# First attention of a two-block model on one core: order of a step, place of the heads' output, running sums as two float32r matmuls

## The reference, cut to what matters

```
h   = w[cond] applied to x over the 32 tokens          # (64, 32, 256)
q,k = rope(h Wq'), rope(h Wk')                          # 16 heads of 128
v,g = h Wv', h Wg'
s   = clip(h Ws1' Ws2' + b, -32, 32)                    # 16 heads x 64 slots
z   = cumlogsumexp(s over tokens);  es = exp(s);  enz = exp(-z)
A   = causal(q k') / sqrt(128)
ok  = enz * (A es)
p   = softmax(ok);   W2 = causal((p*enz) es')
o   = W2 v;   o = o / sqrt(mean(o*o) + eps) * gn * silu(g)
x   = x + o Wo'
```

## Time and profile before

| | us |
|---|---|
| runs of the kernel | 1489.26, 1491.48, 1494.16; median 1491.48 |
| the profiled execution, its own time | 1494.37 |
| its span, first to last instruction | 1492.5 |
| busy in the span: TensorE / VectorE / ScalarE / GpSimd | 1361.8 / 918.0 / 507.1 / 514.6 |
| mean granted TensorE clock | 0.968 |

### The profile page before, as it was taken

One profiled execution on the slowest core, in us unless ns is written; L12 is line 12 of the kernel. 1 busy time (PEld: TensorE's weight loads), 2 busy tenths in 40 slices (PEclk: granted clock), 3 DMA queues, 4 the chain that ended last, 5 costly groups with the idle time before them and its releaser, 6 DMA issues. The chain is left out here.

```text
span 1492.5 us, 46698 instructions
## 1 busy us (share of the span) xinstructions
PE 1361.8 (91%) x19926; PEld 1060.2 (71%) x19926; DVE 918.0 (62%) x1825; ACT 507.1 (34%) x1123; POOL 514.6 (34%) x544
## 2 busy tenths in 40 slices
PE   2999999999999999999996598999999689997996
PEld 2677777777777777777764486777777567775664
DVE  2777777777777777777764465242433335665886
ACT  2344443444443444333342313132322222222332
POOL 0655545555544555544432212221212111122111
PEclk9999999999999999999999699999999879997998
DMA  6000000000001000000000510000000540000620
GB/s 200 9 13 13 14 16 13 27 13 13 13 16 28 13 13 13 3 2 3 2 2 2 201 52 1 0 0 0 0 1 0 167 121 1 0 0 3 197 66 22
DMA packets 33414, 47.57 MB, mean 32 GB/s; under 512 B 6718, under 2 KB 22296, under 8 KB 32728
## 3 DMA queue, kind: packets, MB, share of 16 engines
q1 hardware_dynamic: 31048, 42.69, 9.2%
q10 hardware_dynamic: 2112, 2.10, 0.5%
q0 software_dynamic: 80, 0.26, 0.1%
HBM read 42.68 MB, written 2.36 MB: 30 GB/s over the span
## 5 line engine op out<-in xcount | busy, mean ns | idle before, releaser
L233 POOL TENSOR_TENSOR rstd<-mse,mhalf 128x4 f32<-128x4 f32 x64 | 65.1, 1017 | 238.5 <-DVE mse L651 238.5
L563 ACT ACTIVATE ex<-ok,mn 128x64 f32<-128x64 f32 x256 | 68.2, 337 | 193.7 <-DVE mn L680 193.7
L403 PE MATMUL AW_TA<-w_o,ogT_s 128*128 128x256 f32 x512 | 129.0, 395 | 0.7 <-ACT ogT_s L488 0.7
L822 POOL TENSOR_TENSOR hT_lo<-h,hT_hi 128x512 fp32r<-128x512 f32 x44 | 56.8, 1292 | 192.8 <-ACT hT_hi L995 192.8
L228 POOL TENSOR_TENSOR turned<-t1c,t2s 128x512 f32<-128x512 f32 x62 | 79.8, 1287 | 117.5 <-DVE t2s L611 117.5
L626 DVE SCALAR_TENSOR_TENSOR gs<-gs,PJ 128x512 f32<-128x512 f32 x64 | 44.0, 687 | 122.5 <-ACT gs L504 122.5
L622 DVE RECIPROCAL enz<-SC 128x128 f32<-128x128 f32 x128 | 112.6, 921 | 4.7 <-PE SC L354 4.7
L303 PE MATMUL PJ<-hs_hi,w_hi 128*128 128x512 f32 x248 | 115.2, 464 | 0.0
L1058 DVE SCALAR_TENSOR_TENSOR t<-th,m 128x512 f32<-128x512 f32 (+1 forms) x56 | 38.4, 685 | 121.3 <-ACT th L1000 93.5
L314 PE MATMUL PJ<-w_hi,hs_hi 128*128 128x512 f32 x256 | 111.7, 436 | 0.0
L403 PEld LDWEIGHTS AW_TA<-w_o,ogT_s 128*128 128x128 f32 x512 | 93.0, 191 | 17.2 <-ACT ogT_s L488 1.0
(11 more groups left out here) (378 smaller groups left out, 3440.6 us busy)
## 6 DMA issues: line engine op xcount, KB each, us to landing
we_ring<-in_we SPq DMA_DIRECT2D x64, 256.0 KB, 3.0
w_raw<-in_w_slices SPq DMA_DIRECT2D x48, 128.0 KB, 2.1
turned<-in_w_slices ACTq DMA_DIRECT2D x4, 512.0 KB, 7.6
xres<-in_x SPq DMA_DIRECT2D x2, 1024.0 KB, 14.3
out_rows<-xres SPq DMA_DIRECT2D x16, 128.0 KB, 1.7
w1r<-in_w1i SPq DMA_DIRECT2D x1, 1408.0 KB, 6.7
w_s<-in_w SPq DMA_DIRECT2D x2, 682.0 KB
w_o<-in_wo SPq DMA_DIRECT2D x1, 1024.0 KB, 5.4
```

The lines of the kernel that those rows point to most:

```text
L233: pool.tensor_tensor(rstd[:, :], mse[:, :], mhalf[:, :], ALU.pow).then_inc(o_rstd, 1)
L403: m = pe.matmul(AW[:, 2 * P:2 * P + D], ogT_s[:, h * P:(h + 1) * P], w_o[:, i // G % 2, h, :], start=(h == 0), stop=(h == HQ - 1))
L563: act.activation(ex[:, cols], ok[:, cols], ACT.Exp, scale=-1.0, bias=mn[:, h:h + 1]).then_inc(ok_exp, 1)
L822: eng.tensor_tensor(hT[1][s, m % 2, :], h[s, m % 2, :], hT[0][s, m % 2, :].bitcast(F32), ALU.subtract).then_inc(second, 1)
```

## The change

The edit does this:

- TensorE's order of a step becomes: scores(i), slot_scores(i), slots(i+1), x1(i), x2(i), turn_p(i), turn_og(i-1), the first two heads of heads_out(i-2), slot_weights(i), the other two heads, turn_es(i+1), values(i), running(i+1), proj_v(i+1), proj_g(i+1). values is now of the same step.
- heads_out writes the right half of the bank OE (whose left half is slot_scores') instead of AW; `ogT_s` has two buffers; heads_out waits for `ok_z` and `y_add`, slot_scores for an earlier `y_add`.
- The running sum is two float32r matmuls. ScalarE makes the exponential twice (`es` in fp32, `es_hi` in float32r), GpSimd the rest `es_lo`, before which `running` can't start. `m01_r` is a copy of `m01`.
- The tables of cosine and sine are 32 columns wide, repeated over the 16 sequences by a step of zero.
- ScalarE: squares of the same step, after the copy of the transposed es. VectorE: og's product and the sum of squares at the end of the same step, between the two reciprocals; the mask of the scores is first. GpSimd: norm(i) last. In the prologue the low part of the first es stands before the last rotation.

```diff
@@ buffers
+        m01_r = sb("m01_r", [P, P], F32R)
+        es_hi = sb("es_hi", [P, SW], F32R)
+        es_lo = sb("es_lo", [P, SW], F32R)
-        ogT_s = sb("ogT_s", [P, QW])
+        ogT_s = sb("ogT_s", [P, 2, QW])
@@ gpsimd
+            def slots_low(i):
+                pool.wait_ge(s_first, i + 1)
+                pool.wait_ge(cum_mm, i)
+                pool.tensor_tensor(es_lo[:, :], es[:, :], es_hi[:, :].bitcast(F32), ALU.subtract).then_inc(s_second, 1)
+
             for j in range(QUAD):
+                if j == QUAD - 1:
+                    slots_low(0)
                 rotate(j)
...
             for i in range(STEPS):
-                if i >= 1:
-                    norm(i - 1)
                 pool.wait_ge(ok_exp, HQ * (i + 1))
                 pool.wait_ge(pT_tr, i)
                 pool.tensor_tensor(exz[:, :], ex[:, :], enz[:, :], ALU.mult).then_inc(p_z, 1)
+                if i < LAST:
+                    slots_low(i + 1)
...
-            norm(LAST)
+                norm(i)
@@ tensor
             def running(i):
-                pe.wait_ge(s_exp, i + 1)
-                pe.matmul(SC[:, SW:2 * SW], m01[:, :], es[:, :], start=True, stop=True).then_inc(cum_mm, 1)
+                pe.wait_ge(s_second, i + 1)
+                pe.matmul(SC[:, SW:2 * SW], m01_r[:, :], es_hi[:, :], start=True, stop=False)
+                pe.matmul(SC[:, SW:2 * SW], m01_r[:, :], es_lo[:, :], start=False, stop=True).then_inc(cum_mm, 1)
@@
             def slot_scores(i):
                 pe.wait_ge(a_mask, i + 1)
                 pe.wait_ge(ok_z, i)
+                pe.wait_ge(y_add, i - 2) if i >= 3 else None
@@
-            def heads_out(i):
-                pe.wait_ge(ogT_ev, i + 1)
-                pe.wait_ge(a_mask, min(i + 3, STEPS))
-                pe.wait_ge(wo_scaled, i // G + 1)
-                for h in range(HQ):
-                    m = pe.matmul(AW[:, 2 * P:2 * P + D], ogT_s[:, h * P:(h + 1) * P], w_o[:, i // G % 2, h, :],
+            def heads_out(i, part=(0, HQ)):
+                if part[0] == 0:
+                    pe.wait_ge(ogT_ev, i + 1)
+                    pe.wait_ge(y_add, i)
+                    pe.wait_ge(ok_z, min(i + 3, STEPS))
+                    pe.wait_ge(wo_scaled, i // G + 1)
+                for h in range(*part):
+                    m = pe.matmul(OE[:, SW:SW + D], ogT_s[:, i % 2, h * P:(h + 1) * P], w_o[:, i // G % 2, h, :],
...
             for i in range(STEPS):
                 more = i < LAST
-                if i >= 1:
-                    values(i - 1)
                 scores(i)
-                x1(i)
+                slot_scores(i)
                 if more:
                     slots(i + 1)
-                slot_scores(i)
-                if i >= 2:
-                    heads_out(i - 2)
+                x1(i)
                 x2(i, A)
                 turn_p(i)
+                if i >= 1:
+                    turn_og(i - 1)
+                if i >= 2:
+                    heads_out(i - 2, (0, 2))
+                slot_weights(i)
+                if i >= 2:
+                    heads_out(i - 2, (2, HQ))
+                if more:
+                    turn_es(i + 1)
+                values(i)
                 if more:
                     running(i + 1)
-                if i >= 1:
-                    turn_og(i - 1)
-                if more:
                     proj_v(i + 1, A)
-                slot_weights(i)
-                if more:
-                    turn_es(i + 1)
                     proj_g(i + 1, A)
-            values(LAST)
@@ scalar
             def s_e(i):
                 act.wait_ge(s_clip, i + 1)
+                act.wait_ge(s_second, i)
                 act.activation(es[:, :], sclip[:, :], ACT.Exp).then_inc(s_exp, 1)
+                act.wait_ge(cum_mm, i)
+                act.activation(es_hi[:, :], sclip[:, :], ACT.Exp).then_inc(s_first, 1)
@@ vector, the four products of x1 and x2
+            def turned_by(out_, bank, table):
+                by = "p (b t) -> p b t"
+                return dve.tensor_tensor(out_.rearrange(by, t=T), bank[:, :].rearrange(by, t=T),
+                                         table[:, :].unsqueeze(1).to_broadcast([P, TOK // T, T]), ALU.mult)
@@ vector, the loop
             for i in range(STEPS):
-                silu(i)
-                if i >= 1:
-                    gated(i - 1)
                 dve.wait_ge(a_mm, i + 1)
                 dve.wait_ge(ok_mm, i)
                 dve.tensor_tensor(by_pairs(am), both, for_heads(mA), ALU.mult).then_inc(a_mask, 1)
-                if i >= 1:
-                    norm_sum(i - 1)
+                silu(i)
...
-                if i >= 2:
-                    y_out(i - 2)
...
-                if more:
-                    z(i + 1, 0)
-                    z(i + 1, 1)
                 dve.wait_ge(w2_mm, i + 1)
                 dve.wait_ge(o_mm, i)
                 dve.tensor_tensor(by_pairs(wm), both, for_heads(m01_own), ALU.mult).then_inc(w2_mask, 1)
+                if i >= 2:
+                    y_out(i - 2)
+                if more:
+                    z(i + 1, 0)
+                gated(i)
+                norm_sum(i)
+                if more:
+                    z(i + 1, 1)
             y_out(LAST - 1)
-            gated(LAST)
-            norm_sum(LAST)
             y_out(LAST)
```

More of the change, by code:

```diff
@@ L64, in attention0 @@
         gn_col = sb("gn_col", [P, 1])
-        cosb = sb("cosb", [P, TOK])
-        sinb = sb("sinb", [P, TOK])
+        cosb = sb("cosb", [P, T])
+        sinb = sb("sinb", [P, T])
         mA = sb("mA", [P, T])
@@ L110, in attention0 @@
         s2_raw = [t2c[0:RW, :], t2s[0:RW, :]]
-        products = [(t1c[:, :], t1s[:, :], t2c[:, :], t2s[:, :]), (gs[:, 1, :], og[:, :], sq[:, :], ogT_s[:, :])]
+        products = [(t1c[:, :], t1s[:, :], t2c[:, :], t2s[:, :]), (gs[:, 1, :], og[:, :], sq[:, :], ogT_s[:, 0, :])]
         scratch = nc.dram_tensor("chosen_rows", (B, TW), F32, kind="Internal").ap()
@@ L160, in attention0 @@
         s_clip, s_exp, z_rec = sem("s_clip"), sem("s_exp"), sem("z_rec")
+        s_first, s_second, m01_in = sem("s_first"), sem("s_second"), sem("m01_in")
         a_mm, a_mask = sem("a_mm"), sem("a_mask")
@@ L395, in turn_og @@
                 turn(TB, og, HQ, ogT_tr)
-            def heads_out(i):
-                pe.wait_ge(ogT_ev, i + 1)
-                pe.wait_ge(a_mask, min(i + 3, STEPS))
-                pe.wait_ge(wo_scaled, i // G + 1)
-                for h in range(HQ):
-                    m = pe.matmul(AW[:, 2 * P:2 * P + D], ogT_s[:, h * P:(h + 1) * P], w_o[:, i // G % 2, h, :],
+            def heads_out(i, part=(0, HQ)):
[6 more added lines that the diff above has]
+                    m = pe.matmul(OE[:, SW:SW + D], ogT_s[:, i % 2, h * P:(h + 1) * P], w_o[:, i // G % 2, h, :],
                                   start=(h == 0), stop=(h == HQ - 1))
-                m.then_inc(y_mm, 1)
+                if part[1] == HQ:
+                    m.then_inc(y_mm, 1)
             def turn_p(i):
@@ L413, in slot_weights @@
                 pe.wait_ge(esT_ev, i + 1)
-                pe.wait_ge(y_add, i - 1) if i >= 2 else None
                 for a in range(2):
@@ L453, in _ @@
             pe.wait_ge(ld, 16 * LOADS)
+            pe.wait_ge(m01_in, 1)
             running(0)
@@ L537, in _ @@
                 act.activation(uT[:, n * 512:(n + 1) * 512], bank[0:RW, :], ACT.Identity, bias=u_col[:, 0:1]).then_inc(u_high, 1)
+            act.activation(m01_r[:, :], m01[:, :], ACT.Copy).then_inc(m01_in, 1)
             s_e(0)
@@ L548, in ogT_out @@
             def ogT_out(i):
-                act.wait_ge(y_mm, i)
-                copy(ogT_s[:, :], TB[:, :], ogT_tr, i + 1, ogT_ev)
+                act.wait_ge(y_mm, i - 1) if i >= 2 else None
+                copy(ogT_s[:, i % 2, :], TB[:, :], ogT_tr, i + 1, ogT_ev)
             for i in range(STEPS):
                 more = i < LAST
-                if i >= 1:
-                    square(i - 1)
                 if LEAD + i < STEPS:
@@ L570, in _ @@
                 if more:
+                    esT_out(i + 1)
+                square(i)
+                if more:
                     v_out(i + 1)
-                    esT_out(i + 1)
                     g_t(i + 1)
-            square(LAST)
             ogT_out(LAST)
@@ L602, in x1_by_cos @@
                 dve.wait_ge(qk_add, j if j >= QUAD else max(j - 1, 0))
-                dve.tensor_tensor(products_of(j)[0][:, :], banks_of(j)[0][:, :], cosb[:, :], ALU.mult).then_inc(x1_cos, 1)
+                turned_by(products_of(j)[0][:, :], banks_of(j)[0], cosb).then_inc(x1_cos, 1)
             def x1_by_sin(j):
-                dve.tensor_tensor(products_of(j)[1][:, :], banks_of(j)[0][:, :], sinb[:, :], ALU.mult).then_inc(x1_sin, 1)
+                turned_by(products_of(j)[1][:, :], banks_of(j)[0], sinb).then_inc(x1_sin, 1)
             def x2_by_both(j):
                 dve.wait_ge(x2_mm, j + 1)
```

(10 more changed lines are left out.)

## The result

| | us |
|---|---|
| before, median of 4 runs | 1490.47 (1489.26 to 1494.16) |
| changed, median of 4 runs | 1525.41 (1522.79 to 1526.71) |
| ratio changed to before | 1.0225, 95% interval 1.0208 to 1.0243 |
| profiled executions, before and changed | 1494.37 and 1522.79; spans 1492.5 and 1521.0 |

The changed kernel is slower by 2.25%: 33.5 us by the ratio, 34.9 by the medians, and 28.5 by the two traces. Forecast were 1519 and 27.5 more.

The account below looks back on a forecast made before the run. TensorE, busy all the time at full clock, was taken as the bound: 58 steps x 0.43 = 24.9, plus 2.6 at the ends, 27.5 us on the median 1491.5: 1519. Range 1500 to 1532, with two tenths outside.

Parts of the forecast that it names:

- The mask's wait: Between scores and slot_scores, TensorE waits for VectorE's mask: 0.59 us added a step, bounds 0.45 to 0.75.
- The running sum: Two float32r matmuls take 0.24 us instead of 0.43 in fp32: gain 0.19 a step, bounds nothing to 0.22.
- No gain from the joined runs: x1 with x2, and v with g, as runs of 12 projection matmuls keep 0.231 us each: no new pace.
- rival A: x2's surplus 0.18 us is an fp32-to-float32r switching price, similar at v and g; joining saves 0.35 a step: 1499; 8 in 100.
- Rival B: Besides rival A's saving, the two runs of 12 close up to 0.213 us a matmul: 1474; 7 in 100 with other hidden gains.
- The step: Steady step on TensorE: 12.23 us against 11.80, 0.43 more.
- The tie at turn_p: turn_p's inputs ready at 4.84 us after scores' first matmul, TensorE arriving at 4.85; a late answer costs up to 0.2.
- rival C: turn_p's chain 0.2 us late, or VectorE's queue holds the mask: 0.65 to 0.8 a step, 1532 to 1540; 12 in 100.
- The ends: Late steps +3.3 us; prologue, steps 0 and 1, and tail together -0.7; in all +2.6.
- Now only the wait does, so they last as long as the others: Steps 60 to 62, without x1 and x2: TensorE waits before turn_p, 3 x 1.1 = +3.3 us.
- The prologue: GpSimd's low half ahead of the last rotation starts that rotation at about 57.0, and scores(0) waits for it: +1.8 us.
- The tail: After the last values the gating no longer waits for the y before it: about -1.5 us.

Follow-up runs that it names:

- Experiment 1: Changed kernel, but slot_scores reads the masked scores of the step before, so it doesn't wait for this step's mask (output not the model's): 1507.5 us, ratio to before 1.0095.
- experiment 4: Changed kernel with the running sum as one fp32 matmul again, everything else kept: 1537.7 us, ratio to before 1.0310.
- experiment 9: Kernel before, with only the running sum as two float32r matmuls, placed behind turn_og, order otherwise old: 1480.8 us against 1490.0, ratio 0.9939.
- experiment 8: Kernel before, with heads_out moved behind x2, so x2 no longer follows fp32 matmuls: 1491.0 us against 1490.0, ratio 1.0006.
- experiment 3: Changed kernel with slots and x1 put back between scores and slot_scores: 1600.3 us, ratio to before 1.0743, from two runs.
- experiment 6: Changed kernel with 48 useless projection matmuls added, steps 60 to 63 repeating x1 and x2 of earlier steps: 1516.0 us, ratio to before 1.0172.
- experiment 7: Changed kernel, with steps 60 to 63 running heads_out in one piece ahead of turn_p, no work added: 1513.1 us, ratio to before 1.0146.
- experiment 2: As Experiment 1, with VectorE's silu also moved from ahead of ok to behind the clip: 1521.6 us, ratio to before 1.0209.
- experiment 5: Changed kernel with heads_out in one piece ahead of slot_weights instead of split: 1531.7 us, ratio to before 1.0275.

## Why the prediction was right, point by point

**The mask's wait** was the right mechanism and place. Its size was 1.28 for scores with the round trip; it is 1.15, outside the 1.2 to 1.35 that the prediction wanted to see, and at its lower bound of 0.45 for the wait. I had taken the answer of W2's mask from the earlier trace rows whole, where VectorE starts 0.37 after the last small matmul has started (805.38 to 805.75); here it is 0.23 (421.01 to 421.24). Experiment 1 shows 0.46 for it on the spot.

**The running sum**: 0.19 forecast; 0.20 and 0.22 by experiments 4 and 9.

**No gain from the joined runs**: right. The run of twelve goes at 0.228, as the earlier trace rows had it, and rival A is refuted by experiment 8. Rival B, a pace near 0.213, isn't seen in any kernel. The Trainium skill, "TensorE: Matmul & The Clock Gate", Back-to-back issue gap, has 131 ns for such a stream of 512-column matmuls; no run of six, twelve or 22 here comes below 226, so for this kind of operand the trace does not agree.

**The step**: 12.23 forecast, 12.14 measured; the difference is the mask's 0.13, less some 0.05 at turn_p. Over scores(0) to scores(60) 23.9 were forecast (58 steps and the first two), 18.5 came.

**The tie at turn_p**: right as a tie. The profile lists no wait in the steady step, but turn_p and its second transpose come some 0.08 late (0.53 against 0.45, behind experiment 9). That it binds showed fully as soon as the mask's wait was gone or covered (experiments 1 and 3), and rival C's size never came.

**The ends** were the step that failed. "Now only the wait does, so they last as long as the others" was +3.3; it was +8.7. I had the idle 2.6 us in my hands, since it is the 3.56 of the earlier trace rows less slot_scores and slots, and had seen the clock hold at 1.00 over shorter ones, and didn't ask what a single long one does. The wait itself was about right: with steps of 12.13, as in experiment 6, the three would be 3.1 longer than before. The other 5.6 is the low clock. Experiments 6 and 7 give back 9.5 and 12.3 us by filling the idle piece. The prologue was +0.5 instead of +1.8: turn_es does wait for the delayed rotation, but everything before it had started 1.2 earlier in this execution (the last of the 24 projection matmuls at 41.12, and at 42.36 before), so the delay itself is as forecast. The tail was +0.6 instead of -1.5: the heads of step 63 ran at the low clock too, which is some 1.5 of it (1.40 and 2.00 to the next group instead of 0.96 each).

The two errors, -5.4 in the steady steps and +5.4 at the late ones, cancelled: the traces' 28.5 against 27.5 is closer than its terms, and that was luck. By the ratio and the medians the loss is 5 to 6 us more than in the two traces; the profiled execution before was the slowest of its four runs and the changed one the fastest of its four. One place where single executions differ shows in the prologue (last section); that it makes up the 5 us isn't shown.

## What to carry to other kernels

Where one engine is full, an instruction order is a plan of covers: list every answer that comes from another engine (here the mask, 0.46 beyond scores, and the chain to the transposes, 3.56) and what stands in front of it. Joining work that was spread out saves only real seams, here none, and takes covers away. And a step that misses part of its work at the end of a loop needs an order of its own, or the wait costs its length and can cost the clock besides.

## What was not expected of the hardware

In the late steps of the kernel before, TensorE's granted clock stayed at 1.00 with idle pieces of 0.7 and 1.1 us in each:

```profile
782.04 0.44 PE L358 MATMUL AW_TA<-ident,exz 128*128 128x128 f32 x2 [1.10 <-POOL exz L262]
```

It also stayed at 1.00 in experiment 3, with 1.3 us in every step. In the changed kernel it fell after the piece of 2.6 us at 786 to 789, and the step with it took 14.7 instead of 12.1. It fell as well in the first late step of experiments 1 to 5, which have pieces of 2.6 to 2.9.

The length of one piece doesn't settle it, though. In experiment 2 the second late step has the same piece, and the clock stayed at 1.00 (timeline, then the stretch from 800 to 810 us); that step took 11.66, the ones beside it 13.21 and 13.18:

```profile
804.57 0.44 PE L370 MATMUL AW_TA<-ident,exz 128*128 128x128 f32 x2 [2.59 <-POOL exz L271]
```

```profile
800.00:810.00 10.00, 7.41 (x185) 5.69 (x184) 5.05 (x11) 4.24 (x11) 3.45 (x4) 1.00 0.01 3
```

A shorter piece can be enough too. In the prologue of the new order TensorE is idle for 1.8 to 2.0 us in front of turn_es (0.56 before). In the profiled executions of experiments 1, 2, 4 and 5 the clock was low behind it, 0.57 to 0.62 from 58 to 66 us, and the first step took 12.9 to 13.3; in those of the changed kernel and of experiments 6 and 7 it was 1.00, and the first step took 11.0. This is the stretch in experiment 5:

```profile
58.00:66.00 8.00, 6.84 (x110) 5.38 (x111) 3.84 (x8) 2.67 (x9) 4.98 (x6) 0.57 0.06 19
```

What decides between the two isn't shown here. The Trainium skill, "TensorE: Matmul & The Clock Gate", What's actually happening, says that the gate goes by how busy TensorE has been of late and knows two levels; the traces agree, with 0.96 and 1.84 us for the same four instructions.
